# Unused identity transposes on TensorE at the entry of four stages of a four-layer language tower

## The chip, the cores and the metric

The kernel runs on one core of a Trainium2 chip. The metric is the device time of one execution in microseconds (us), the median of several runs. A core has five engines with queues of their own: PE (TensorE, with its weight loads shown as PEld), DVE (VectorE), ACT (ScalarE), POOL (GpSimd) and SP (SyncE, which here only starts transfers). They wait for each other through semaphores.

## The reference

256 tokens of 16 sequences pass through four layers, each a mixing part and a feed-forward part, with a residual around each (the first stage is an embedding with a convolution of nine taps over token ids):

```python
h = tok(x, emb, W, b)                                  # embedding and 9-tap convolution
h = h + linear_attention(layernorm(h))                 # L0
h = h + routed_ffn(layernorm(h))
h = h + batchnorm_attention(layernorm(h))              # L1
h = h + gelu_moe(layernorm(h), hidden=128, top2 of 8)
h = h + window_attention(layernorm(h))                 # L2
h = h + gelu_moe(layernorm(h), hidden=64, top2 of 8)   # keeps its input too
h = h + rational_convolution(layernorm(h))             # L3, by Fourier transforms
h = h + depth_ffn(layernorm(h))                        # upper half of the tokens by a router's weight
```

Shapes are (16, 256, 64) throughout, in fp32. The expert stages compute, for every token, a router's eight logits, keep the two largest with softmax weights, and add the two experts' outputs `gelu(x @ W1[e] + b1[e]) @ W2[e] + b2[e]`, weighted.

## The kernel before

The activations stay in one SBUF tensor `H`, as 8 chunks of 2 sequences x 256 tokens. Stages run one after the other (`tower`, the loop over `stages`, L2554), each in a block of its own with one queue of instructions per engine; between two blocks all engines meet at a barrier (L2563). PSUM is four tensors `PS[0..3]` of two banks each. Within a stage the order is written out by hand: semaphores carry every dependency, and what an engine does next is what its queue holds next.

**Expert stages** (`gelu_moe`, called as m1 with hidden 128, `again=True`, and as m2 with hidden 64, `again=False`). Each works in two rounds of four chunks. TensorE's queue opens with waits for the weights, for ScalarE's `sel` and for VectorE's `identb` and `b2_split` (L1271 to L1275). Then come, for the first round, `turn_x` twice (L1209: four 128x128 transposes of the normalised input each, with ScalarE's copy L1159 or L1162 between and after), `logits` (L1220: sixteen matmuls of 16 columns), `hidden(0)` and `hidden(1)` (L1237), `turn_parts` (L1226) and `gates(0)` (L1245). VectorE starts the stage with five small operations that split `b2` and one cast that makes `identb` (L1119), and then waits for the logits, from which a chain of 18 short operations (`Gating`, L966 to L991) makes the gates. From then on the loop over `steps` runs: gates (L1245), hidden (L1237), output (L1257, L1261), with ScalarE's Gelu (L1184) and VectorE's product (L1137) between. The banks: `hid_bank` is banks 0 to 2, `gate_bank` 3 and 4, `y_bank` 5 and 6, `ahead_bank` 7; `y_bank[1]` is first used by the second pair of chunks.

**Rational convolution.** TensorE waits for its weights and for VectorE's `nyq` (L2007), makes one transpose (L2008) that ScalarE copies (L1952) ahead of its sixteen L1954, and then waits for `coef` (L1871, a VectorE product). The loop of L2011 follows: four matmuls L2019 and L2022 (coefficients) and two L2030 (transform of the input) per step; ScalarE's L1965, L1966 and L1974 and VectorE's L1898 to L1906 take them up.

**Last stage** (`depth_ffn`). Its normalisation isn't prepared by the stage before: VectorE's statistics (L132 to L144), GpSimd's power (L150), VectorE's L156 and L166 come first. TensorE waits for `normed`, then runs, per round of four chunks, transposes L2242, router weights L2250, hidden L2258, output L2266, transposes L2275; ScalarE takes L2250's result with L2218, and VectorE ranks the tokens (L2160 to L2176) from it.

`C["ident"]` is the 128x128 identity in fp32, in SBUF since the start of the kernel (group `base`). `L2563` in the rows stands for the barrier between blocks, `PEq`, `DVEq`, `POOLq` for the engines' sequencers.

Of the kernel before, what the change touches and what calls it, by code (L numbers as in the profile page):

```python
# [21 lines left out]
P = 128  # L22
# [75 lines left out]

class NormBuffers:
# [902 lines left out]
def gelu_moe(nc, H, PS, C, dram, pre, hid, again):  # L1006
# [5 lines left out]
    with ExitStack() as ctx:  # L1012
# [20 lines left out]
        banks = [PS[k // 2][:, k % 2, :] for k in range(2 * W)]  # L1033
        hid_bank, gate_bank, y_bank, ahead_bank = banks[0:3], banks[3:5], banks[5:7], banks[7]
# [162 lines left out]
        def _(pe):  # L1197
            ident = C["ident"]
            w1 = C[pre + "_w1"].rearrange("p (s n) -> p s n", s=SL)
            w2 = C[pre + "_w2"].rearrange("p (s f) -> p s f", s=SL)  # L1200

            def turn_x(it, k):
                for w in (2 * k, 2 * k + 1):
                    pe.wait_ge(S["normed"], it * W + w + 1)
                    if k:
                        pe.wait_ge(S["xT"], it * 2 + 1)
                    for u in range(U):
                        at = (w % 2 * U + u) * P
                        ins = nc.tensor.transpose(ahead_bank[:, at:at + P],  # L1209
                                                  xn[:, w, 2 * u:2 * u + 2, :].rearrange("p g f -> p (g f)"), ident)  # L1210
                ins.then_inc(S["xT_ps"], 1)
# [566 lines left out]
def rational_convolution(nc, H, PS, C, dram):  # L1778
    with ExitStack() as ctx:
# [29 lines left out]
        banks = [PS[k // 2][:, k % 2, :] for k in range(2 * W)]  # L1809
# [189 lines left out]
        def _(pe):  # L1999
            ident = C["ident"]  # L2000
# [2 lines left out]
            odd = C["rat_odd"].rearrange("p (c n) -> p c n", c=2)  # L2003
            back = C["rat_back"].rearrange("p (t c u n) -> p t c u n", t=2, c=2, u=U)
            pe.wait_ge(C.sem("base"), C.count("base"))
            pe.wait_ge(C.sem("rat"), C.count("rat"))
            pe.wait_ge(S["nyq"], 7)  # L2007
            nc.tensor.transpose(banks[4][0:PAIRS, 0:P], nyq[:, 0], ident).then_inc(S["nyq_ps"], 1)  # L2008
# [31 lines left out]
            for m in range(PAIRS):  # L2040
# [4 lines left out]
                bank = banks[m % 8]  # L2045
# [9 lines left out]
            for l in range(LT):  # L2055
                bank = banks[l // 8 % 8]
# [45 lines left out]
def depth_ffn(nc, H, PS, C, dram):  # L2102
    with ExitStack() as ctx:
# [19 lines left out]
        @block.sync  # L2123
        def _(sp):

            ov = C.out.rearrange("(h c) (u p) f -> u h p c f", h=2, u=U)
            hv = H[:].rearrange("p (c u h f) -> p u h c f", c=CHUNKS, u=U, h=2)
            for r in range(ITERS):
                sp.wait_ge(S["h_new"], (r + 1) * W)
                for u in range(U):  # L2130
                    for half in range(2):
                        c = slice(r * W, (r + 1) * W)
                        sp.dma_start(ov[u, half][:, c], hv[:, u, half, c]).then_inc(S["stored"], 16)
            sp.wait_ge(S["stored"], 16 * U * 2 * ITERS)
# [95 lines left out]
        @block.tensor  # L2230
        def _(pe):
            ident = C["ident"]
            w1 = C["dep_w1"].rearrange("p (s h n) -> p s h n", s=SLABS, h=2)
            w2 = C["dep_w2"].rearrange("p (s f) -> p s f", s=SLABS)
            wr = C["dep_wr"].rearrange("p (h n) -> p h n", h=2)
            pe.wait_ge(C.sem("dep"), C.count("dep"))

            def one_round(it, first):
                for w in range(W):
                    pe.wait_ge(S["normed"], it * W + w + 1)  # L2240
                    for u in range(U):
                        ins = nc.tensor.transpose(PS[w][:, 0, u * P:(u + 1) * P],  # L2242
                                                  xn[:, w, 2 * u:2 * u + 2, :].rearrange("p g f -> p (g f)"), ident)
                    ins.then_inc(S["xT_ps"], 1)
                for w in range(W):
                    pe.wait_ge(S["xT"], it * W + w + 1)
                    if not first:
                        pe.wait_ge(S["ys"], (it - 1) * W + w + 1)
                    for half in range(2):
                        ins = nc.tensor.matmul(PS[w][:, 1, half * T:(half + 1) * T], wr[:, half, :], xT[:, w],  # L2250
                                               start=True, stop=True)
                    ins.then_inc(S["wb_ps"], 1)
                for w in range(W):
                    for s in range(SLABS):
                        if s == 1:
                            pe.wait_ge(S["wb"], it * W + w + 1)
                        for half in range(2):
                            ins = nc.tensor.matmul(PS[w][:, s, half * T:(half + 1) * T], w1[:, s, half, :], xT[:, w],  # L2258
                                                   start=True, stop=True)
                        ins.then_inc(S["hid0_ps"] if s == 0 else S["hid1_ps"], 1)  # L2260
                for w in range(W):
                    pe.wait_ge(S["hid0"], it * W + w + 1)
                    pe.wait_ge(S["hid1"], it * W + w + 1)
                    for half in range(2):
                        for s in range(SLABS):
                            ins = nc.tensor.matmul(PS[w][half * D:(half + 1) * D, 0, 0:T], w2[:, s, :],  # L2266
                                                   hid[:, w, s, half * T:(half + 1) * T], start=(s == 0),
                                                   stop=(s == SLABS - 1))
                    ins.then_inc(S["yT_ps"], 1)
                for w in range(W):  # L2270
                    pe.wait_ge(C.sem("base"), C.count("base"))
                    pe.wait_ge(S["yT"], it * W + w + 1)
                    for u in range(U):
                        at = slice(u * P, (u + 1) * P)
                        ins = nc.tensor.transpose(PS[w][:, 1, at], yT[:, w, at], ident)  # L2275
                    ins.then_inc(S["y_ps"], 1)

            one_round(0, True)
            with pe.Fori(1, ITERS) as it:
                one_round(it, False)  # L2280
# [306 lines left out]
```

## Time and profile before

| | us |
|---|---|
| median of 3 runs | 940.95 |
| lowest and highest run | 935.21 and 942.48 |
| the profiled execution's own time | 940.95 |
| its span, first to last instruction | 939.1 |
| PE busy | 696.9 (74%) |
| DVE busy | 517.8 (55%) |
| ACT busy | 341.9 (36%) |
| mean granted clock of TensorE | 0.813 of 2.4 GHz |

The page gives, per engine, busy time and its share of the span. The granted clock is that of TensorE alone and has two levels here, 0.50 (1.2 GHz) and 1.00 (2.4 GHz). In timelines an entry is: start, length, engine, line, operation, tensors, shape, count, and in brackets how long the engine sat idle before it and what released it. Matmuls are pipelined: their starts are recorded and their ends are modelled, so several in a row take less than the sum of their durations. An fp32 matmul of the program is two instructions in the trace, except for a transpose, which is one.

### The profile page before, as it was taken

The numbers are of one execution on the slowest core, as the hardware profiler recorded it, in microseconds if no ns is written. First come the engines' busy times: TensorE is split into PE (matmuls) and PEld (weight loads), VectorE is DVE, ScalarE is ACT, GpSimd is POOL, SyncE is SP. The second block draws the span as 40 slices with busy tenths as digits, with TensorE's granted clock in tenths as the row PEclk, the third lists the DMA queues.
The fourth block names the chain that finished last, engine by engine and source line by source line (L and its number), as shares of the span: only waits on it lengthen the run. The fifth ranks groups of instructions, "written<-read, shape, count | busy, mean of one in ns | idle before, by whom it ended". The sixth has DMA issues, their size and how long they took to land. (4 is left out here: it accounts for less than half of the span.)

```text
span 939.1 us, 13121 instructions
## 1 busy us (share of the span) xinstructions
PE 696.9 (74%) x4499; PEld 466.5 (50%) x4499; DVE 517.8 (55%) x1359; ACT 341.9 (36%) x620; POOL 217.1 (23%) x195
## 2 busy tenths in 40 slices
PE   2687667978882699984767777747876978999674
PEld 1565555647661323233656666633322645886453
DVE  0144883444547556752455545327375799444597
ACT  1232112425451245442333332212334967433253
POOL 6421110130201010102344434122013566000320
PEclk9899777988996599995667666555887999999788
DMA  8652221000000100000000000033000000000001
GB/s 278 177 158 76 77 63 59 2 1 1 1 1 0 60 1 1 1 14 22 6 6 6 7 6 6 6 116 138 0 1 31 1 0 1 1 2 1 1 21 26
DMA packets 18988, 32.31 MB, mean 34 GB/s; under 512 B 6482, under 2 KB 15730, under 8 KB 18162
## 3 DMA queue, kind: packets, MB, share of 16 engines
q1 hardware_dynamic: 16370, 22.11, 7.5%
q0 software_dynamic: 2560, 9.44, 3.2%
q8 instruction: 35, 0.57, 0.2%
q14 instruction: 23, 0.19, 0.1%
HBM read 29.54 MB, written 1.05 MB: 33 GB/s over the span
## 5 line engine op out<-in xcount | busy, mean ns | idle before, releaser
L150 POOL TENSOR_TENSOR norm_rstd<-norm_var,minus_half 128x16 f32<-128x16 f32 x16 | 47.1, 2942 | 367.2 <-DVE norm_var L144 367.2
L1184 ACT ACTIVATE m_g<-PS,w_slot 128x512 f32<-128x512 f32 x96 | 60.7, 685 | 72.2 <-PE PS L1237 65.9
L1137 DVE TENSOR_TENSOR m_gw<-m_g,PS 128x512 f32<-128x512 f32 x96 | 61.4, 683 | 41.8 <-PE PS L1245 29.6
L1237 PE MATMUL PS<-m_xT,w_slot 64*128 64x512 f32 x192 | 71.4, 702 | 6.9 <-ACT m_g L1184 6.8
L1261 PE MATMUL PS<-m_gw,w_slot 128*64 128x512 f32 x192 | 57.7, 671 | 0.0
L246 PE MATMUL PS<-w_base,tok_windows 128*128 128x128 f32 x128 | 22.0, 347 | 28.1 <-DMA tok_windows<-in_emb,tok_ids 18.5
L1409 POOL TENSOR_TENSOR win_rms<-win_ms,win_minus_half 128x24 f32<-128x24 f32 x8 | 33.3, 4167 | 37.4 <-DVE win_ms L1467 37.4
L1974 ACT COPY rat_xf<-PS 64x512 f32 x32 | 33.7, 1052 | 5.4 <-PE PS L2030 5.2
L1245 PE MATMUL PS<-m_gT,m_sel 48*128 48x512 bf16 x96 | 24.2, 425 | 15.3 <-DVE m_gw L1137 9.6
L226 POOL DMA_INDIRECT tok_windows<-in_emb,tok_ids x32 | 30.5, 952 | 21.5 <-PE PS L257 9.2
L1696 PE MATMUL PS<-win_v,win_probT 64*128 64x65 f32 x256 | 29.7, 405 | 7.5 <-ACT win_probT L1588 6.5
L246 PEld LDWEIGHTS PS<-w_base,tok_windows 128*128 128x128 f32 x128 | 19.9, 182 | 29.8 <-issue 16.2
L132 DVE BATCH_NORM_STATS2 norm_halves<-H 128x6 f32<-128x64 f32 x256 | 33.9, 210 | 0.9 <-PEq L2563 0.9
L2050 PE MATMUL PS<-w_slot,rat_ht 128*128 128x256 f32 x128 | 34.1, 391 | 0.0
L1464 DVE TENSOR_REDUCE win_ms<-win_sq 128x24 f32<-128x1536 f32 x8 | 14.0, 1753 | 35.6 <-ACT win_sq L1565 35.6
L1696 PEld LDWEIGHTS PS<-win_v,win_probT 64*128 64x128 f32 x256 | 28.0, 318 | 11.1 <-ACT win_probT L1588 9.5
L1237 PEld LDWEIGHTS PS<-m_xT,w_slot 64*128 64x128 f32 x192 | 24.3, 218 | 18.1 <-ACT m_g L1184 14.9
L2030 PE MATMUL PS<-w_slot 128*128 128x512 f32 x64 | 31.3, 613 | 0.3 <-DVE w_slot L1888 0.3
L1245 PEld LDWEIGHTS PS<-m_gT,m_sel 48*128 48x128 bf16 x96 | 5.4, 94 | 51.0 <-DVE m_gw L1137 27.8
L1261 PEld LDWEIGHTS PS<-m_gw,w_slot 128*64 128x64 f32 x192 | 10.3, 142 | 37.1 <-DVE m_gw L1137 26.4
L1906 DVE RECIPROCAL rat_hf<-rat_hf 128x256 f32<-128x256 f32 x16 | 27.9, 1741 | 0.0
L1920 DVE COPY rat_hf<-PS 128x512 f32 x16 | 16.6, 1040 | 20.0 <-PE PS L2050 20.0
(327 smaller groups left out, 1656.8 us busy)
## 6 DMA issues: line engine op xcount, KB each, us to landing
rff_routed<-in_routed SPq DMA_DIRECT2D x64, 129.0 KB, 2.1
rat_hf<-in_rat_den SPq DMA_DIRECT2D x1, 2048.0 KB, 7.6
rat_hf<-in_rat_num SPq DMA_DIRECT2D x1, 2048.0 KB, 13.5
w_slot<-in_w_rat SPq DMA_DIRECT2D x1, 1716.5 KB, 17.0
w_slot<-in_w_win SPq DMA_DIRECT2D x1, 1378.5 KB, 5.9
w_slot<-in_w_m SPq DMA_DIRECT2D x1, 1329.0 KB, 6.1
w_slot<-in_w_early SPq DMA_DIRECT2D x1, 1156.0 KB
out<-H SPq DMA_DIRECT2D x8, 128.0 KB, 2.2
```

The lines of the kernel that those rows point to most:

```text
L132: ins = nc.vector.bn_stats(N.st[:, w * G4 + g, :], x_of(w)[:, g, :])
L150: nc.gpsimd.tensor_tensor(N.rstd[:], N.var[:], C.minus_half[:], ALU.pow).then_inc(S["norm_rstd"], 1)
L246: ins = nc.tensor.transpose(PS[w][:, k, g * P:(g + 1) * P], win[:, slot(it, w), g, at:at + P], ident)
L1137: nc.vector.tensor_tensor(gw[:, i % 2, half, :], g[:, i % 2, half, :], gate_bank[half], ALU.mult)\
L1184: nc.scalar.activation(g[:, i % 2, half, :], hid_bank[(n - 1) % 3], ACT.Gelu, bias=b1[:, s:s + 1])\
L1237: nc.tensor.matmul(hid_bank[n % 3], w1[lane(half), s, :], pair_of(xT, pair)[lane(half)], start=True, stop=True).then_inc(S["hid_ps"], 1)
L1261: ins = nc.tensor.matmul(y[half], w2[:, s, :], gw[:, i % 2, half, :], start=False, stop=(s == SL - 1))
L1409: nc.gpsimd.tensor_tensor(rms[:, c % W], ms[:, c % W], minus_half[:], ALU.pow).then_inc(S["rms"], 1)
L1696: ins = nc.tensor.matmul(PS[w][:, i, g * DV:(g + 1) * DV], probT[rows[i], c % 2, half * (BLOCKS // 2) + g, :], (v if par else v2)[rows[i], ...
L1974: ins = nc.scalar.copy(dst, banks[4 + s % 4][rows, :].rearrange("p (t x l) -> p t x l", t=2, x=2))
L2030: ins = nc.tensor.matmul(banks[4 + s % 4], xd[:, w, 2 * u + half].rearrange("p a f -> p (a f)"), dft[:, u, :], start=(u == 0), stop=(u == ...
L2050: ins = nc.tensor.matmul(bank[:, 2 * LT:], part_of[c], odd[:, c, :], start=(c == 0), stop=(c == 1))
```

## The change

A helper `rouse` issues `count` transposes of the identity, each 128x128 fp32, into the first 128 columns of a bank that nothing uses at that time. They carry no semaphore, nothing reads their output, and they are issued in TensorE's queue ahead of the waits of the stage: 24 in the first expert stage, 44 in the second, 16 in the rational convolution (behind the wait for `base`, which is long met), 36 in the last stage. Nothing is removed or moved on any engine.

```diff
+def rouse(nc, C, bank, count):
+
+    for _ in range(count):
+        nc.tensor.transpose(bank[:, 0:P], C["ident"], C["ident"])
...
             w2 = C[pre + "_w2"].rearrange("p (s f) -> p s f", s=SL)
+            rouse(nc, C, y_bank[1], 24 if again else 44)
...
             pe.wait_ge(C.sem("base"), C.count("base"))
+            rouse(nc, C, banks[7], 16)
             pe.wait_ge(C.sem("rat"), C.count("rat"))
             pe.wait_ge(S["nyq"], 7)
...
             wr = C["dep_wr"].rearrange("p (h n) -> p h n", h=2)
+            rouse(nc, C, PS[3][:, 1, :], 36)
             pe.wait_ge(C.sem("dep"), C.count("dep"))
```

## Rows read from the trace of the kernel before

**Rows 1.** The page, part 1: busy us (share of the span) and instructions.

```profile
PE 696.9 (74%) x4499; PEld 466.5 (50%) x4499; DVE 517.8 (55%) x1359; ACT 341.9 (36%) x620; POOL 217.1 (23%) x195
```

**Rows 2.** The chain that ended last, last stage: start, us, what.

```profile
875.69 3.30 issue
...
879.03 3.03 POOL norm_rstd L150
...
885.40 5.31 PE PS L2250 x16
```

**Rows 3.** Timeline, PE, before and at the entry of the first expert stage.

```profile
294.14 4.14 PE L923 MATMUL PS<-w_base,bna_junk 128*128 128x128 f32 x16 [1.72 <-ACT bna_junk L835]
307.80 1.09 PE L1209 MATMUL PS<-w_base,norm_xn 128*128 128x128 f32 x4 [9.52 <-DVE m_identb L1119]
...
311.80 3.60 PE L1220 MATMUL PS<-w_slot,m_xT 128*128 128x16 f32 x16 [0.87 <-ACT m_xT L1159]
```

**Rows 4.** Timeline, DVE, entry of the first expert stage.

```profile
305.79 0.53 DVE L1076 CAST m_b2b<-w_slot 128x64 bf16<-128x64 f32 x1 [0.98 <-PEq L2563]
```

**Rows 5.** Timelines, DVE and PE, entry of the second expert stage.

```profile
626.18 0.54 DVE L1076 CAST m_b2b<-w_slot 128x64 bf16<-128x64 f32 x1 [1.59 <-PEq L2563]
...
629.95 1.09 PE L1209 MATMUL PS<-w_base,norm_xn 128*128 128x128 f32 x4 [5.86 <-DVE m_identb L1119]
```

**Rows 6.** Timeline, PE, other places: transposes and L1220 at either clock.

```profile
27.20 5.29 PE L246 MATMUL PS<-w_base,tok_windows 128*128 128x128 f32 x24 [2.99 <-DMA tok_windows<-in_emb,tok_ids]
38.45 3.68 PE L246 MATMUL PS<-w_base,tok_windows 128*128 128x128 f32 x16 [5.96 <-DVE tok_windowsT L302]
...
58.72 7.21 PE L246 MATMUL PS<-w_base,tok_windows 128*128 128x128 f32 x64 [0.77 <-DVE H L310]
...
660.36 0.66 PE L1209 MATMUL PS<-w_base,norm_xn 128*128 128x128 f32 x4
...
669.09 1.96 PE L1220 MATMUL PS<-w_slot,m_xT 128*128 128x16 f32 x16
```

**Rows 7.** Stretches: length, busy PE, PEld, DVE, ACT, POOL; then PEclk.

```profile
42.51:97.00 54.49, 45.71 (x327) 33.22 (x325) 24.52 (x78) 16.71 (x38) 11.56 (x10) 1.00 0.42 117
...
298.51:301.90 3.39, 0.00 (x0) 0.00 (x0) 3.29 (x20) 0.00 (x0) 1.53 (x1) 1.00 0.00 0
301.92:332.62 30.70, 19.37 (x58) 8.92 (x60) 16.59 (x67) 7.89 (x11) 4.78 (x3) 0.50 0.12 46
...
673.97:680.77 6.80, 4.83 (x10) 1.51 (x10) 2.16 (x5) 3.75 (x5) 0.00 (x0) 0.50 0.00 0
...
800.27:878.75 78.48, 70.02 (x793) 56.23 (x792) 34.28 (x84) 27.68 (x41) 0.00 (x0) 1.00 0.01 1
878.77:888.99 10.22, 6.05 (x17) 4.54 (x18) 7.66 (x33) 2.31 (x6) 7.51 (x6) 0.50 0.01 2
```

**Rows 8.** Timelines, DVE, PE and ACT, start of the rational convolution.

```profile
719.03 0.83 DVE L1859 TENSOR_TENSOR rat_hf<-w_slot 128x288 f32<-128x288 f32 x2 [1.10 <-PEq L2563]
...
721.69 0.37 PE L2008 MATMUL PS<-w_base,rat_nyq 128*32 128x128 f32 x1 [4.48 <-DVE rat_nyq L1869]
726.11 2.07 PE L2019 MATMUL PS<-rat_hf,w_slot 128*128 x4 [4.05 <-DVE rat_hf L1871]
...
722.60 8.42 ACT L1954 ACTIVATE rat_xf<-w_slot 128x512 f32<-128x512 f32 x16
...
732.85 1.05 ACT L1974 COPY rat_xf<-PS 64x512 f32 x1 [0.56 <-PE PS L2030]
```

**Rows 9.** Timeline, PE, first round of the last stage.

```profile
882.73 1.80 PE L2242 MATMUL PS<-w_base,norm_xn 128*128 128x128 f32 x6 [8.53 <-DVE norm_xn L166]
...
890.54 7.07 PE L2258 MATMUL PS<-dep_xT,w_slot 128*128 128x256 f32 x32
```

**Rows 10.** Timeline, PE, one step of the first expert stage, early and later.

```profile
326.00 1.20 PE L1245 MATMUL PS<-m_gT,m_sel 48*128 48x512 bf16 x2 [0.85 <-DVE m_gw L1137]
...
332.16 0.60 PE L1245 MATMUL PS<-m_gT,m_sel 48*128 48x512 bf16 x2
...
400.06 0.39 PE L1245 MATMUL PS<-m_gT,m_sel 48*128 48x512 bf16 x2
...
403.02 0.39 PE L1245 MATMUL PS<-m_gT,m_sel 48*128 48x512 bf16 x2
```

## The prediction

> **What bounds the kernel now.** I read four views, in this order. The page's busy shares first [rows 1]: the reader is to see that no engine is busy throughout; TensorE, the busiest, is at 74% and VectorE at 55%. So the kernel is a row of stages, each with its own chain of waits, and what TensorE's speed is worth has to be read stage by stage. Second, the chain that ended last [rows 2]. It reaches back only to the entry of the last stage; there TensorE counts with the sixteen L2250 matmuls (5.31 us), behind GpSimd's power (L150, 3.03 us). Third, the timelines at the four entries where the new work goes [rows 3, 4, 5, 8, 9]: what TensorE waits for there, and until when. Fourth, the granted clock by stretch [rows 7]: 1.00 is 2.4 GHz and 0.50 is 1.2 GHz. TensorE starts the first expert stage in a stretch of 0.50 that lasts from 301.92 to 332.62 us, though its real work begins at 307.80; the first round of the last stage falls into another, 878.77 to 888.99. The second expert stage starts at the low clock too: its L1209 takes the same 1.09 us [rows 3, 5].
>
> **What each transpose costs.** The new instruction is a 128x128 fp32 transpose, the form of L246 and L1209. 24 of L246 in a row took 5.29 us at the low clock and 64 took 7.21 us at the high one [rows 6]. The last one's pipeline overhangs, so I subtract L1209's four, 1.09 us cold [rows 3] and 0.66 fast [rows 6]: (5.29 - 1.09)/20 = 0.21 us each at 1.2 GHz, (7.21 - 0.66)/60 = 0.11 us each at 2.4 GHz.
>
> Do such transposes raise the clock? The L246 run that begins at 38.45 [rows 6] is followed by the high clock from 42.51 on [rows 7], 4.1 us later; and sixteen L923, from 294.14 to 298.28 [rows 3], are followed by 1.00 in 298.51:301.90 [rows 7]. Before both, TensorE had been idle or nearly so. So a run does raise it, some 4.1 to 4.4 us after it begins. And it does not stay: in 298.51:301.90 TensorE does nothing, and at 301.92 the clock is back at 0.50.
> The Trainium skill (TensorE: Matmul & The Clock Gate, Part 4: PE-mode transpose) says the opposite, that transposes don't engage the full clock. By that rule nothing would be gained anywhere and the sum would be rival B's; the two runs above contradict it.
>
> **First expert stage (24).** All engines enter at about 305.8 (VectorE's first row [rows 4]). Today TensorE waits until 307.80, for VectorE's small casts that end with m_identb [rows 3]. So 2.0 us of the new work is covered, the rest delays L1209. Bounds: all 24 cold are 24 x 0.21 = 5.0 us, 3.0 past the cover; all fast are 2.6 us, 0.6 past it. By the rise above I take 4.1 us cold (19 or 20 transposes) and 5 x 0.11 = 0.55: 4.6 us, +2.6 us. What is queued behind is all of it: L1209, ScalarE's copy, L1209 again, L1220, and then VectorE's gate chain, which can't start before L1220. Against that, what runs at the high clock right after: twice four L1209, 1.09 to 0.66 us, 2 x 0.43 = 0.86; sixteen L1220, 3.60 to 1.96 us [rows 3, 6], 1.64. Together 2.5 us. Net +0.1 us; +3.0 - 0.86 = +2.1 if the clock rises late and falls before L1220.
> Then, from the end of L1220 at 315.4 [rows 3] to the gates' work at 326.00 [rows 10], TensorE has little beside VectorE's gate chain, and I expect the clock to fall. The rows say so: in the second expert stage L1220 ran fast at 669.09 (1.96 us) [rows 6], two L1237 followed, and the stretch 673.97:680.77 is at 0.50 [rows 7]. So the PE-bound first step, 326.00 to 332.16 [rows 10], stays as slow as it is.
>
> **Second expert stage (44).** The entry is at 626.2, the real L1209 at 629.95 [rows 5]: 3.8 us of cover, more because VectorE's casts are slower here. 4.1 us cold (19) and 25 x 0.11 = 2.75 make 6.85 us, +3.05 past the cover. Bounds: 44 x 0.21 = 9.2 us, +5.4; all fast 4.8 us, +1.0. Gain: the same L1209, 0.86, and L1220, up to 1.64. L1220 begins some 3 us after L1209, with TensorE half idle between; I take half of it here, 0.8. Net +3.05 - 1.7 = +1.3 us.
>
> **Convolution (16).** Entry at 719.0 [rows 8]. 16 x 0.21 = 3.4 us, to 722.4; the transpose L2008 stood at 721.69, so it comes 0.7 us late. Behind it wait ScalarE's copy and its sixteen L1954, which run from 722.60 for 8.42 us without a gap; ScalarE had 0.56 us idle before L1974 at 732.85 [rows 8]. 0.7 - 0.56 = 0.15 us late, which the small gaps of the next steps take up. TensorE's own next work waits for VectorE until 726.11 [rows 8], so it idles again, as it did before the fall at 301.92. Even with the clock held, ScalarE is the one that sets the first step, so the gain is at most those 0.56 us. I take 0; bounds -0.56 and +0.7.
>
> **Last stage (36).** The clock is at 1.00 until 878.75 [rows 7] and the entry is at about 875.7 [rows 2], so the run begins fast: 36 x 0.11 = 4.0 us, to 879.7. If the clock fell inside, at most 36 x 0.21 = 7.6 us, to 883.3, 0.6 past the first L2242 at 882.73 [rows 9]. Cover: GpSimd's power and VectorE's L166. I take 0 for the cost. Gain: the chain holds L2250 with 5.31 us; at the high clock sixteen would take half of L2258's 7.07 us for 32 [rows 9], 3.5, so at most 1.8 us. But 3 us idle follow, and then L2242 in pairs, each waiting for VectorE. By the 301.92 fall I expect the low clock to be back before L2250: 0 here, bound -1.8.
>
> **Sum.** +0.1 + 1.3 + 0 + 0 = +1.4 us on the profiled execution's own 940.95 us (span 939.1 and 1.85 around it; it is also the median of the three): 942.4 us.
>
> **Rivals.**
> (A) The clock holds once raised. Then the first step of both expert stages is fast as well: 326.00 to 332.16 is 6.2 us, the same work from 400.06 to 403.02 is 3.0 us [rows 10], 3.2 us each. First stage +0.1 - 3.2, second +3.05 - 2.5 - 3.2 = -2.65, convolution -0.56, last -1.8: -8.1 us, 932.8. For it: the work after a run is not nothing. Against it: the fall at 301.92 and the one at 673.97. A part of it, one stretch of the four, gives 938 to 941.
> (B) The clock isn't raised, because the operand is the identity, mostly zeros, where L246 and L923 carried data. Then +3.0 and +5.4 for the expert stages and +0.15 for the convolution, nothing in the last stage: +8.6 us, 949.5. It decides as soon as the spacing of the new transposes stays at 0.21 us to their end. For it: no row shows an identity on both sides; against it: the runs of [rows 3, 6]. The Trainium skill (TensorE: Matmul & The Clock Gate, Part 4: PE-mode transpose) would bring the same.
> (C) The clock rises, but falls before L1220: first stage +2.1, second +3.05 - 0.86 = +2.2, convolution +0.7: +5.0 us, 946.0. For it: TensorE is half idle between the two L1209 groups and L1220, which wait for ScalarE's copies.
> Where a rise or a fall comes isn't fixed to the program, and the three runs of before differ by 7.3 us; so each term has a scatter of a us or two that I can't sign.
>
> **How the numbers follow.** Forecast (+1.4, with small shifts either way, 938 to 944.5) 0.56; a part of A 0.14; A itself 0.07; C 0.15; B 0.08. The range that holds 8 in 10 takes in the forecast, part of A and most of C: 936 to 947. 1% is 9.4 us, about what a measurement of this kernel can tell from no change. Faster by over that (under 931.5) needs all of A and more: 0.06. Slower (over 950.4) needs B with a scatter on top: 0.05. Within: 0.89.
>
> **What would show it.** L1209's first start moves some 2.6 us after the new run's cover in the first expert stage and 3 in the second; the spacing of the new transposes falls from 0.21 to 0.11 within the run; L1209's four take 0.66 and L1220 about 2 us; the stretch before the first PE-bound step is at 0.50 again. In the convolution L2019's first instruction stays 7.1 us after the entry. In the last stage L2250 still takes over 4.6 us. I am wrong if the clock reads 1.00 when the gates (L1245) begin, if L2250 takes 3.5 us, or if the new run never speeds up.

## The result and the profile after

The changed kernel takes 936.06 us (median of 20 runs) against 940.45 us for the kernel before (20 runs of its own beside them): a ratio of 0.9961, 95% interval [0.9943, 0.9979]. The medians differ by 4.4 us, a small gain, just inside the predicted range (by 0.1 us) but on the other side of the kernel before than the forecast (+1.4 us). The ratio, which leaves out two slow executions of the changed kernel (1000.33 and 3367.49 us), isn't the quotient of the medians (0.9953): it stands for 3.7 us. The profiled execution takes 936.7 us (span 934.9), 4.2 less than the one before. The mean granted clock is 0.836, before it was 0.813.

The page of the changed kernel, part 1, and two groups of part 5 (line, operation, busy us and mean ns of one, then idle time before them and what ended it). L1244 and L1268 were L1237 and L1261 before: the helper and its calls moved the later lines by 6 to 9.

```profile
PE 700.0 (75%) x4619; PEld 475.3 (51%) x4619; DVE 516.7 (55%) x1359; ACT 341.6 (37%) x620; POOL 217.8 (23%) x195
...
L1244 PE MATMUL PS<-m_xT,w_slot 64*128 64x512 f32 x192 | 68.3, 667 | 7.6 <-ACT m_g L1190 7.5
L1268 PE MATMUL PS<-m_gw,w_slot 128*64 128x512 f32 x192 | 55.7, 649 | 0.0
```

The same groups of the kernel before, part 5 of its page.

```profile
L1237 PE MATMUL PS<-m_xT,w_slot 64*128 64x512 f32 x192 | 71.4, 702 | 6.9 <-ACT m_g L1184 6.8
L1261 PE MATMUL PS<-m_gw,w_slot 128*64 128x512 f32 x192 | 57.7, 671 | 0.0
```

There are 120 instructions more, the new ones, and nothing else differs [rows 1]. These two groups, which both expert stages share, became 5.1 us shorter on TensorE (3.1 and 2.0); the stretches below show more of the work at the high clock.

The first question is where. I take the length of a stage from one barrier to the next, in each profiled execution (us). The mark is the moment at which GpSimd clears the semaphores inside the barrier, about half a us ahead of the stage's first rows:

| kernel | up to 1st expert | 1st expert | window attention | 2nd expert | convolution | last |
|---|---|---|---|---|---|---|
| before | 305.2 | 114.9 | 205.4 | 93.0 | 156.8 | 63.4 |
| changed | 307.1 | 114.2 | 202.9 | 90.9 | 158.1 | 61.4 |

Up to the first expert stage the change touches nothing; its +1.9 is scatter between executions. The window attention has no new work and is 2.5 us shorter; the convolution is 1.3 longer. Timeline of PE in the changed kernel, entries of the four stages.

```profile
307.66 4.26 PE L106 MATMUL PS<-w_base 128*128 128x128 f32 x24 [7.51 <-PEq L2572]
311.76 0.60 PE L1216 MATMUL PS<-w_base,norm_xn 128*128 128x128 f32 x4
...
314.82 1.96 PE L1227 MATMUL PS<-w_slot,m_xT 128*128 128x16 f32 x16 [0.87 <-ACT m_xT L1165]
...
327.38 1.20 PE L1252 MATMUL PS<-m_gT,m_sel 48*128 48x512 bf16 x2 [0.85 <-DVE m_gw L1143]
...
624.72 6.64 PE L106 MATMUL PS<-w_base 128*128 128x128 f32 x44 [2.09 <-PEq L2572]
631.19 0.60 PE L1216 MATMUL PS<-w_base,norm_xn 128*128 128x128 f32 x4
...
633.86 2.66 PE L1227 MATMUL PS<-w_slot,m_xT 128*128 128x16 f32 x16 [0.68 <-ACT m_xT L1168]
...
645.67 0.61 PE L1252 MATMUL PS<-m_gT,m_sel 48*128 48x512 bf16 x2 [1.51 <-DVE m_gT L1096]
...
715.48 1.94 PE L106 MATMUL PS<-w_base 128*128 128x128 f32 x16 [1.82 <-PEq L2572]
...
722.57 2.07 PE L2027 MATMUL PS<-rat_hf,w_slot 128*128 x4 [4.16 <-DVE rat_hf L1878]
...
873.63 4.12 PE L106 MATMUL PS<-w_base 128*128 128x128 f32 x36 [1.63 <-PEq L2572]
880.54 1.80 PE L2251 MATMUL PS<-w_base,norm_xn 128*128 128x128 f32 x6 [2.78 <-DVE norm_xn L172]
882.99 4.17 PE L2259 MATMUL PS<-dep_xT,w_slot 128*128 128x256 f32 x16
```

L106 is the new run; the reader is to see how long it takes (24 in 4.26 us, 44 in 6.64), that what follows at once is fast (L1216 in 0.60, 1.09 before [rows 3]) and that the first gates' work at 327.38 is as slow as before, 1.20 us for two L1252 [rows 10]. Stretches of the changed kernel in the two expert stages (length, then busy PE, PEld, DVE, ACT, POOL, then PEclk):

```profile
310.80:317.40 6.60, 4.77 (x39) 4.06 (x38) 0.47 (x2) 1.55 (x2) 0.00 (x0) 1.00 0.25 105
317.55:334.50 16.95, 12.59 (x32) 3.44 (x31) 12.63 (x53) 5.29 (x8) 2.90 (x1) 0.50 0.00 1
...
628.12:634.90 6.78, 5.34 (x48) 4.89 (x46) 0.00 (x1) 1.17 (x2) 0.00 (x0) 1.00 0.99 425
634.97:651.98 17.01, 13.38 (x36) 5.05 (x37) 13.05 (x55) 5.29 (x8) 1.21 (x1) 0.50 0.31 133
...
658.85:662.20 3.35, 3.35 (x11) 1.32 (x10) 0.00 (x0) 0.51 (x2) 0.00 (x0) 0.50 0.00 0
...
675.95:682.70 6.75, 6.12 (x14) 2.17 (x16) 2.31 (x5) 2.42 (x4) 0.00 (x0) 0.50 0.00 0
682.75:716.70 33.95, 25.80 (x127) 8.51 (x124) 22.39 (x64) 11.65 (x19) 4.17 (x2) 1.00 0.02 3
```

The high clock won by the new run is gone at 317.5 and at 635.0, before the PE-bound part of either stage begins. But the second stage's later half, from 682.75 to its end at 715.5, runs at 1.00 throughout. Stretches of the kernel before, same columns, same part of the second expert stage:

```profile
687.63:691.02 3.39, 3.39 (x10) 0.50 (x8) 1.25 (x2) 1.35 (x3) 0.00 (x0) 0.50 0.02 5
691.04:701.25 10.21, 7.86 (x40) 2.31 (x38) 6.94 (x30) 4.27 (x7) 0.59 (x1) 1.00 0.00 0
701.28:708.08 6.80, 6.80 (x16) 1.77 (x16) 4.34 (x9) 1.85 (x3) 2.29 (x1) 0.50 0.00 0
```

Here the clock is at 0.50 twice, 10.2 us in all (3.4 and 6.8), and TensorE is busy through both. In both kernels a long low stretch ends 27.3 us into the stage. From there to the stage's end it had 17.0 us at 0.50 before (these and the 6.8 of [rows 7]) and has 10.1 after (658.85 and 675.95). 6.9 us less at half speed, where TensorE is the limit, are worth up to 3.4 us; the gates begin 0.8 later; the stage is 2.1 shorter. So the time is found. What brought it there, 50 us behind the new work, is the question for the experiments.

### The profile page after: what moved, and what is told of

Its sections match the earlier page's. It is cut to its first block and busy times, and to the rows that moved or that the text cites. A ratio compares the mean times of both kernels' runs of the same rounds, so it can differ in the third digit from the quotient of the medians.

```text
span 934.9 us, 13361 instructions
## 1 busy us (share of the span) xinstructions
PE 700.0 (75%) x4619; PEld 475.3 (51%) x4619; DVE 516.7 (55%) x1359; ACT 341.6 (37%) x620; POOL 217.8 (23%) x195
## 5 line engine op out<-in xcount | busy, mean ns | idle before, releaser
L1143 DVE TENSOR_TENSOR m_gw<-m_g,PS 128x512 f32<-128x512 f32 x96 | 61.3, 683 | 38.1 <-PE PS L1252 24.5
L1244 PE MATMUL PS<-m_xT,w_slot 64*128 64x512 f32 x192 | 68.3, 667 | 7.6 <-ACT m_g L1190 7.5
L1268 PE MATMUL PS<-m_gw,w_slot 128*64 128x512 f32 x192 | 55.7, 649 | 0.0
L252 PE MATMUL PS<-w_base,tok_windows 128*128 128x128 f32 x128 | 21.2, 339 | 29.2 <-DMA tok_windows<-in_emb,tok_ids 18.4
L1252 PE MATMUL PS<-m_gT,m_sel 48*128 48x512 bf16 x96 | 24.5, 418 | 16.6 <-DVE m_gw L1143 10.8
L232 POOL DMA_INDIRECT tok_windows<-in_emb,tok_ids x32 | 30.5, 952 | 21.9 <-PE PS L263 9.4
L1703 PE MATMUL PS<-win_v,win_probT 64*128 64x65 f32 x256 | 27.2, 378 | 8.1 <-ACT win_probT L1595 7.1
L1244 PEld LDWEIGHTS PS<-m_xT,w_slot 64*128 64x128 f32 x192 | 23.7, 211 | 18.1 <-ACT m_g L1190 15.3
L1703 PEld LDWEIGHTS PS<-win_v,win_probT 64*128 64x128 f32 x256 | 25.6, 292 | 11.2 <-ACT win_probT L1595 9.6
L1252 PEld LDWEIGHTS PS<-m_gT,m_sel 48*128 48x128 bf16 x96 | 5.6, 94 | 50.2 <-DVE m_gw L1143 32.9
L1268 PEld LDWEIGHTS PS<-m_gw,w_slot 128*64 128x64 f32 x192 | 10.2, 139 | 35.4 <-DVE m_gw L1143 24.4
```

The source lines that it names most:

```text
L252: ins = nc.tensor.transpose(PS[w][:, k, g * P:(g + 1) * P], win[:, slot(it, w), g, at:at + P], ident)
L1143: nc.vector.tensor_tensor(gw[:, i % 2, half, :], g[:, i % 2, half, :], gate_bank[half], ALU.mult)\
L1244: nc.tensor.matmul(hid_bank[n % 3], w1[lane(half), s, :], pair_of(xT, pair)[lane(half)], start=True, stop=True).then_inc(S["hid_ps"], 1)
L1268: ins = nc.tensor.matmul(y[half], w2[:, s, :], gw[:, i % 2, half, :], start=False, stop=(s == SL - 1))
L1703: ins = nc.tensor.matmul(PS[w][:, i, g * DV:(g + 1) * DV], probT[rows[i], c % 2, half * (BLOCKS // 2) + g, :], (v if par else v2)[rows[i], ...
```

## The experiments

Two theories at the outset. **Warmth:** what the new transposes warm up is paid back, at once or later. **Shift:** the transposes only delay the stage, and the clock then falls over other work; warm or cold doesn't matter, and the sign hangs on the size of the delay. Counts are written (first expert, second expert, convolution, last stage); the changed kernel is (24, 44, 16, 36). Each ratio is against the kernel before on the same chip; where a count is 0, the call stands with 0 in it and issues nothing. The lengths quoted are those of one profiled execution each, by the method above.

**The parts alone.**

```diff
 e1_m1 (24, 0, 0, 0)
-            rouse(nc, C, y_bank[1], 24 if again else 44)
+            rouse(nc, C, y_bank[1], 24 if again else 0)
...
 e2_m2 (0, 44, 0, 0)
-            rouse(nc, C, y_bank[1], 24 if again else 44)
+            rouse(nc, C, y_bank[1], 0 if again else 44)
...
 e4_dep (0, 0, 0, 36)
-            rouse(nc, C, y_bank[1], 24 if again else 44)
+            rouse(nc, C, y_bank[1], 0 if again else 0)
...
```

> Only the first expert stage has its 24 transposes. Theory 1: the stage takes about 114.2 instead of 114.9 us, ratio 0.9990 to 0.9995. Theory 2 (the recorded sum): +0.1 us, 115.0 us. The two hardly differ in the time; they differ in whether the first product of the gates (L1245) starts earlier or later after the entry: 20.2 us before, 19.7 after.

Measured: 940.05 against 942.04 us, ratio 0.9975 [0.9951, 0.9999]. First expert stage 114.8, window attention 205.8 us: its trace shows no gain. That execution took 942.80 us at a mean granted clock of 0.812, and seven of the other eleven had 0.826 to 0.833, so what made the median smaller isn't in this trace.

> Only the second expert stage has its 44 transposes. Theory 1 (local gain as between the two profiles): the stage takes about 91 instead of 93 us, ratio about 0.998. Theory 2 (the recorded sum): L1209 starts 2.5 to 3 us later than entry + 3.8, L1209 and L1220 give back 1.7 to 2.5 of it, the stage takes 93 to 94.5 us and the ratio is 1.000 to 1.0015.

Measured: 940.18 against 942.04, 0.9981 [0.9959, 1.0004]. Second expert stage 90.9, convolution 158.1, last stage 61.3 us: the three lengths of the changed kernel, though the convolution and the last stage have no new work here. This execution took 935.03 us, the second fastest of its twelve.

> Only the last stage has its 36 transposes. Theory 1 (gain is real and local: the clock rises earlier in the stage that has the new work): the last stage, 63.4 us in the profile before and 61.4 in the one after, takes 61 to 62 us, L2250's sixteen take about 4.2 instead of 5.3 us, and the whole is 1.5 to 2.5 us faster (ratio 0.9975 to 0.9985). Theory 2 (the recorded one: the clock falls before L2250, the difference of the two profiles is where rises happen to come): the stage scatters around 63 us and the ratio's interval holds 1.

Measured: 942.52 against 942.04, 1.0003 [0.9986, 1.002]. Last stage 63.4 us, as before. PE timeline of e4_dep, entry of the last stage:

```profile
880.96 4.12 PE L106 MATMUL PS<-w_base 128*128 128x128 f32 x36 [1.63 <-PEq L2572]
887.87 1.80 PE L2251 MATMUL PS<-w_base,norm_xn 128*128 128x128 f32 x6 [2.78 <-DVE norm_xn L172]
890.32 5.50 PE L2259 MATMUL PS<-dep_xT,w_slot 128*128 128x256 f32 x16
```

A stretch of e4_dep behind the new run:

```profile
887.35:894.10 6.75, 6.04 (x17) 4.52 (x18) 6.05 (x28) 2.29 (x6) 4.46 (x5) 0.50 0.00 1
```

Thirty-six transposes in 4.12 us, 2.8 us idle, and the clock is at 0.50 when L2251 begins. And e2_m2, with no new work in this stage, has the short L2259 of the changed kernel (PE timeline of e2_m2):

```profile
878.88 1.80 PE L2251 MATMUL PS<-w_base,norm_xn 128*128 128x128 f32 x6 [8.53 <-DVE norm_xn L172]
881.34 4.17 PE L2259 MATMUL PS<-dep_xT,w_slot 128*128 128x256 f32 x16
```

What follows: the transposes of the last stage do nothing that a profile shows. Those of the convolution were never run alone, but it takes 158.1 us with them (changed) and without them (e2_m2). The lengths of both stages come from something that happens ahead of them. By the medians the two expert parts carry the gain, each about half (-2.0 and -1.9 us), though e2_m2's interval still holds no change at all and that of e1_m1 ends just short of it.

**Cold filler of the same place.** To part warmth from delay, the body of the helper becomes a matmul of 16 columns, which is two instructions of 0.21 us. TensorE is as busy as in the cold part of the real run; in the traces of these three kernels the clock stayed at 0.50 through it in the expert stages.

```diff
-        nc.tensor.transpose(bank[:, 0:P], C["ident"], C["ident"])
+        nc.tensor.matmul(bank[:, 0:16], C["ident"], C["ident"][:, 0:16], start=True, stop=True)
 e5_narrow (10, 15, 6, 12); e10_shift11 (0, 11, 0, 0); e11_shift13 (0, 13, 0, 0)
```

> All four places have filler of about the same length in time, but made of matmuls of 16 columns (10, 15, 6 and 12 of them, each two instructions of about 0.21 us cold). In the trace before, sixteen such instructions (L1220) in a row were not followed by the high clock. Theory 1 (the clock is what gains): no rise after the filler, L1209 and L1220 stay slow, both expert stages lose about 2.3 and 2.6 us, and the whole is 4 to 6 us slower than before (ratio 1.004 to 1.006). Theory 3 (something else gains, such as a place in the queue or a moved instruction load): about as fast as the changed kernel, 0.996.

Measured: 944.94 against 942.04, 1.0032 [1.0012, 1.0052]. PE timeline of e5_narrow, first expert stage:

```profile
308.01 4.42 PE L106 MATMUL PS<-w_base 128*128 128x16 f32 x20 [7.67 <-PEq L2572]
312.27 1.09 PE L1216 MATMUL PS<-w_base,norm_xn 128*128 128x128 f32 x4
316.28 3.60 PE L1227 MATMUL PS<-w_slot,m_xT 128*128 128x16 f32 x16 [0.87 <-ACT m_xT L1165]
```

Nothing is warmed: 1.09 and 3.60 us as in [rows 3]. The two expert stages take 117.0 and 94.3, but the window attention 202.8, the convolution 158.1 and the last stage 61.3, as in the changed kernel. Taken whole, a cold filler costs time. That showed two effects of opposite sign rather than one, so I matched the delay of a single stage, to 0.1 us.

> Only the second expert stage has filler, eleven matmuls of 16 columns (22 instructions, about 4.7 us). They don't raise the clock, and they hold L1216 back by about 0.9 us past the cover of 3.8, so that the gates' first product comes 0.9 us late, as it does with the 44 transposes (0.8). Theory 2 (the delay alone moves the later rounds to where the clock falls less often; the early rise isn't what gains): the stage takes 90.5 to 92 us, the convolution about 158.1 and the last stage 61.3, and the ratio is 0.996 to 0.999 although nothing was warmed. Theory 1 (the early rise of the clock is what gains): the delay is lost, the stage takes 93.5 to 94.3 us, the ratio is 1.000 to 1.003.

Measured: 940.19 against 941.75, 0.9985 [0.9961, 1.001]. PE timeline of e10_shift11, second expert stage:

```profile
626.30 4.84 PE L106 MATMUL PS<-w_base 128*128 128x16 f32 x22 [2.09 <-PEq L2572]
630.99 1.09 PE L1216 MATMUL PS<-w_base,norm_xn 128*128 128x128 f32 x4
634.61 3.60 PE L1227 MATMUL PS<-w_slot,m_xT 128*128 128x16 f32 x16 [0.68 <-ACT m_xT L1168]
647.35 0.61 PE L1252 MATMUL PS<-m_gT,m_sel 48*128 48x512 bf16 x2 [1.51 <-DVE m_gT L1096]
```

The last stretch of that stage in e10_shift11:

```profile
684.45:718.40 33.95, 24.55 (x116) 7.25 (x112) 22.39 (x65) 11.67 (x19) 4.22 (x2) 1.00 0.01 2
```

L1216 and L1227 are cold, yet the gates begin at 647.35, 21.05 us into the stage, against 20.95 in the changed kernel (from VectorE's first row of the stage), and from 684.45 on the clock is at 1.00 to the end. Stages: 90.9, 158.2, 61.4 us. From the second expert stage on that is 310.5 us, 310.4 in the changed kernel and 313.1 before: all of those 2.7 us but 0.1, without a warm transpose. The timed runs agree in size (-1.6 us, beside -1.9 for e2_m2), but neither interval excludes zero: the control is shown in the profiled executions and not by the medians.

> As the run with eleven, with thirteen such matmuls (about 5.6 us, L1216 1.8 us late). Theory 2: another length again, anywhere from 91 to 94.5 us, not eleven's plus 0.9. Theory 1: eleven's plus 0.9 us.

Measured (one execution): 945.48 us. Two matmuls more than e10, the gates at 21.9 us, 0.8 later, and the stage takes 96.4 us, 5.5 more. Stretches of e11_shift13:

```profile
692.40:695.70 3.30, 3.30 (x11) 0.59 (x8) 1.05 (x2) 1.47 (x3) 0.00 (x0) 0.51 0.00 0
...
706.00:712.70 6.70, 6.70 (x16) 1.69 (x15) 4.20 (x9) 1.85 (x3) 2.14 (x1) 0.50 0.00 0
```

The two falls of the kernel before are back, 3.5 us later in the stage.

**Warm runs of other lengths in the second expert stage.** The counts are (0, 24, 0, 0), (0, 34, 0, 0) and (0, 60, 0, 0).

```diff
+            rouse(nc, C, y_bank[1], 0 if again else 24)
+            rouse(nc, C, y_bank[1], 0 if again else 34)
+            rouse(nc, C, y_bank[1], 0 if again else 60)
```

> Only the second expert stage, with 24 instead of 44 transposes: 4.6 us, 0.8 past the cover of 3.8, against 2.7 past it with 44. Theory 1 (what gains is the early rise of the clock; the delay costs): L1216 starts 1.9 us earlier than with 44, the stage is about 1 to 2 us shorter than with 44, 89 to 90 us. Theory 2 (what gains is the place that the later rounds of the stage come to stand at against the clock's rises and falls, which a delay of 0.8 us moves): no such order; the stage jumps to 93 us or more, or stays at 90.9, and convolution and last stage come as 156.8 with 63.4 or as 158.1 with 61.3.

Measured: 938.42 against 941.1, 0.997 [0.9948, 0.9993]. The profiled execution, 934.41 us, is the second fastest of its twelve.

> 34 transposes in the second expert stage alone: by the rate of 0.11 us after the rise L1216 starts 1.1 us earlier than with 44. Theory 2: the length is not 44's minus 1.1; with 24 it was 91.1, with 44 it was 90.9, and a value between them in the count may give 90 as well as 94. Theory 1: 90.0 us or less.

Measured (one execution): 937.38 us.

> 60 transposes in the second expert stage alone: L1216 starts 1.8 us later than with 44, and the clock stays up a stretch longer (L1227 all fast). Theory 2: the length jumps or stays, 90.9 to 95 us. Theory 1: 44's 90.9 plus 1.8 minus at most 0.7, about 92 us.

Measured (one execution): 946.02 us.

PE timelines of the three: the new run, which begins at the stage's entry, and the first gates' work. First e7_m2_24:

```profile
622.40 4.45 PE L106 MATMUL PS<-w_base 128*128 128x128 f32 x24 [2.09 <-PEq L2572]
...
640.46 0.61 PE L1252 MATMUL PS<-m_gT,m_sel 48*128 48x512 bf16 x2 [1.51 <-DVE m_gT L1096]
```

The same of e12_m2_34:

```profile
625.38 5.55 PE L106 MATMUL PS<-w_base 128*128 128x128 f32 x34 [2.09 <-PEq L2572]
...
644.53 0.61 PE L1252 MATMUL PS<-m_gT,m_sel 48*128 48x512 bf16 x2 [1.51 <-DVE m_gT L1096]
```

The same of e13_m2_60:

```profile
627.82 8.38 PE L106 MATMUL PS<-w_base 128*128 128x128 f32 x60 [2.09 <-PEq L2572]
...
649.80 0.61 PE L1252 MATMUL PS<-m_gT,m_sel 48*128 48x512 bf16 x2 [1.51 <-DVE m_gT L1096]
```

Side by side, all the profiled executions (e6, e8 and e14 to e16 are described further down):

| second expert stage | gates begin, us after VectorE's first row | length, us |
|---|---|---|
| none (before, e9, e1, e4) | 20.11 to 20.15 | 92.9 to 93.0 |
| 24 warm (e7, e14) | 18.06, 18.07 | 91.1 |
| 34 warm (e12, e15) | 19.15, 19.18 | 90.9, 90.8 |
| 44 warm (changed, e16, e2, e6) | 20.92 to 20.96 | 90.8 to 90.9 |
| 11 narrow, cold (e10) | 21.05 | 90.9 |
| 44 warm and 14 more (e8) | 21.15 | 94.1 |
| 13 narrow, cold (e11) | 21.89 | 96.4 |
| 60 warm (e13) | 21.98 | 96.4 |
| 15 narrow, cold (e5) | 22.76 | 94.3 |

Delays that agree to 0.1 us give equal lengths, whether the filler was warm or cold (44 and 11 narrow; 60 and 13 narrow), and the length isn't a rising function of the delay. With 24 warm transposes the gates come 2.1 us earlier and the stage is 1.9 us shorter, so they pay for themselves at the gates. Whether the 1.9 us come from that isn't shown: with 34 the gates are 1.0 earlier, with 44 they are 0.8 later, and the stage is no longer for it.

**Both expert stages, and keeping the clock up.** e6 is (24, 44, 0, 0). e8 is e6 with six more transposes ahead of the first wait for Gelu and eight behind the first `turn_parts`, where TensorE is idle, to carry the clock to the gates.

```diff
 e8_fill
+                    if n == 3:
+                        rouse(nc, C, y_bank[1], 6)
...
+            rouse(nc, C, y_bank[1], 8)
```

> The transposes of the two expert stages alone (24 and 44), none in the convolution and the last stage. In the profiles so far the last stage took 63.4 us both without and with its own 36, and 61.3 us with no working filler at all, always together with a convolution of 158.1 us; so its length seems to follow from the stage before. Theory 1 (the expert stages make the whole gain, the last two edits nothing): ratio 0.995 to 0.998, as the changed kernel's 0.9961; second expert stage 90.9, convolution 158.1, last stage 61.3 us. Theory 2 (each of the four edits carries a part): ratio 0.998 to 0.999 and a last stage of 63.4 us.

Measured: 938.39 against 941.1, 0.9964 [0.9936, 0.9993]: the whole gain of the change within the uncertainty, without the convolution's and the last stage's part. PE timeline of e6_experts, first expert stage:

```profile
306.94 5.36 PE L106 MATMUL PS<-w_base 128*128 128x128 f32 x24 [7.67 <-PEq L2572]
312.09 0.87 PE L1216 MATMUL PS<-w_base,norm_xn 128*128 128x128 f32 x4
...
315.41 3.06 PE L1227 MATMUL PS<-w_slot,m_xT 128*128 128x16 f32 x16 [0.87 <-ACT m_xT L1165]
```

In this execution the clock rose only 5.7 us after the run began, all 24 were cold, and the stage took 117.3 us in place of 114.2. The code of the stage is the same, the moment of the rise is another: 3.1 us.

> The expert stages' transposes (24 and 44) and further ones where TensorE idles before the first products of the gates: 6 ahead of the wait for the first Gelu in hidden(1), 8 between turn_parts and the wait for gT. Theory 1 (the clock has fallen by the first PE-bound step, which takes 6.2 us cold and 3.0 fast in the rows of before): the step gets faster by 1 to 3 us in both stages, and the whole is 2 to 6 us faster than with 24 and 44 alone. Theory 2 (there is too little idle time to fill, the transposes delay the Gelu's matmuls): the first step is still slow and both stages lose 0.2 to 1 us each.

Measured: 940.22 against 941.1, 0.9992 [0.9967, 1.0017]. PE timeline of e8_fill, second expert stage (L1254 is its gates' line):

```profile
637.80 1.54 PE L106 MATMUL PS<-w_base 128*128 128x128 f32 x6
...
641.68 1.91 PE L106 MATMUL PS<-w_base 128*128 128x128 f32 x8
643.52 0.61 PE L1254 MATMUL PS<-m_gT,m_sel 48*128 48x512 bf16 x2
644.98 1.20 PE L1254 MATMUL PS<-m_gT,m_sel 48*128 48x512 bf16 x2 [0.85 <-DVE m_gw L1143]
```

The additional ones ran cold and the gates are slow all the same. They delay the gates by 0.2 us, and the stage takes 94.1 us, 3.2 more than in e6. So what the clock did at the gates wasn't mended. Whether the 3.2 us come from the delay alone no run separates, since the fourteen also stand between other work of the stage.

**The kernel before once more, and the counts on one chip.** e9_before has the code of before. e14, e15 and e16 ran together on another chip, where the first stage is some 10 us shorter in every trace: (24, 24, 0, 0), (12, 34, 0, 0), and the changed kernel again.

```diff
+            rouse(nc, C, y_bank[1], 24)
+            rouse(nc, C, y_bank[1], 12 if again else 34)
```

> The kernel before once more, for a second trace of it. Theory 1 (the entry of the second expert stage finds the clock's rises and falls in the same place each time, so that the stage's length is a property of its own code): second expert stage 93.0, convolution 156.8, last stage 63.4 us again, and 114.8 us in the first expert stage. Theory 2 (all stage lengths are drawn by chance): other values, 90.9 us for the second expert stage among them.

Measured (one execution): 938.55 us; expert stages and what follows 114.8, 205.3, 93.0, 156.8, 63.4 us, each within 0.1 of the first profile. The 2.4 us between the two executions of one code lie ahead of the first expert stage (303.1 against 305.2, 2.1 us).

> 24 transposes in both expert stages, none elsewhere. Theory 2 (place against the clock's falls): the second expert stage, convolution and last stage take 91.1, 158.0 and 61.3 us as with 24 there alone, the same 310.4 as with 44; so the ratio is that of the changed kernel, 0.995 to 0.998. Theory 1 (each us of earlier gates is a us gained): the gates start 2.9 us earlier than with 44, ratio about 0.993.

Measured: 925.33 against 930.01 (8 runs), 0.9941 [0.9918, 0.9963]. The stages came as theory 2 has it: the gates of the second expert stage begin 2.9 us earlier than with 44, and it takes 91.1 us all the same. The ratio lies between the two theories and decides neither.

> 12 transposes in the first expert stage and 34 in the second, none elsewhere. 12 take 2.5 us cold, 0.4 past the cover of 2.1, and may or may not raise the clock. Theory 2: first expert stage with window attention 317 or 320 us in the trace, whichever way the gates come to stand; second expert stage on, 310.4 us; ratio 0.995 to 0.999. Theory 1: the first expert stage loses the rise and gains nothing, the second as with 44; ratio 0.998.

Measured: 926.8 against 930.01, 0.997 [0.9951, 0.9988]. The 12 took 2.79 us, and the clock stayed at 0.50 behind them.

> The changed kernel once more, beside the two others on one chip. Theory 2: second expert stage 90.9, convolution 158.1, last stage 61.3 us again; the first expert stage gives 114.2 us with window attention 202.9 where its entry stands to the clock as in the first trace, and other lengths where it doesn't. Theory 1: all stages as in the first trace.

Measured: 928.42 against 930.01, 0.9969 [0.9945, 0.9992]. Again a gain: the medians differ by 1.6 us, the ratio is that of 2.9.

48 transposes in place of 120 do as well within the uncertainty: the two intervals overlap, and the profiled stages of e14 and e16 are equal to 0.3 us each (114.2, 202.8, 91.1, 158.0, 61.3 and 114.2, 202.8, 90.8, 158.2, 61.3), so a lead of e14 isn't shown. With 12 in the first expert stage it stays at 114.9 and the window attention at 204.8.

**The window attention.** It has no edit in any kernel. Nine profiled executions without new work in the first expert stage give it 205.3 to 205.9 us. With 24 transposes there, four of six give 202.6 to 202.9 (changed, e16, e14, e8) and two 205.8 to 205.9 (e1, e6); with the cold filler (e5) it is 202.8, and with 12 transposes (e15) 204.8. A stretch over the whole stage, kernel before:

```profile
420.60:626.10 205.50, 143.72 (x1146) 120.72 (x1146) 91.12 (x189) 59.27 (x105) 71.31 (x63) 0.62 0.03 9
```

The same of the changed kernel:

```profile
421.70:624.60 202.90, 140.17 (x1146) 117.76 (x1146) 90.69 (x189) 59.25 (x105) 71.29 (x63) 0.66 0.03 9
```

The same 1146 instructions, a mean clock of 0.66 in place of 0.62, 3.6 us less on TensorE. That is the largest single term of the changed profile, and nothing in the stage was touched.

## Why the prediction was wrong in sign

**Cost and speed of a transpose.** Right. The spacing fell from 0.21 to 0.11 us within the run, 24 took 4.26 us and 44 took 6.64, where 4.65 and 6.85 were predicted; 44 cold would be 9.2, so rival B is out. One reading under it was not sound: the recorded clock begins at 32.26 us, and so no row shows the low clock for the 24 L246 from 27.20; it was inferred from their spacing. The 24 of e6, at a granted clock of 0.50 throughout, took 5.36 us and bear the 0.21 out. The rise came 3.0 and 3.4 us into the run, earlier than my 4.1, and once, in e6, 5.7. The Trainium skill (TensorE: Matmul & The Clock Gate, Part 4: PE-mode transpose) has it that transposes don't engage the full clock; the trace of the changed kernel disagrees: 1.00 in 628.12:634.90, which sets in 3.4 us into a run of transposes begun at the low clock.

**First expert stage.** L1216 moved by 2.1 us (2.6 predicted); the gates came 0.5 us earlier, where +0.1 was the forecast. With the late rise of e6 they came 1.9 later, near the bound of +2.1.

**Second expert stage, entry.** L1216 moved by 2.7 us (3.05 predicted), L1227 took 2.66 us where 2.8 was assumed, and the gates came 0.8 late, not 1.3. The term was 0.5 too large. The clock fell inside L1227 here, so rival C came half true, and at 0.8 us and not 2.2.

**The clock falls before the PE-bound step.** Right, both times (317.55 and 634.97), and e8_fill couldn't hold it. Rival A, the only way to a large gain that I saw, did not happen. The gain came without it.

**Convolution and last stage at nothing.** Right for the new work as far as the profiles show: e4_dep gives 1.0003, and e2_m2 has the lengths of the changed kernel without it. The 16 transposes took 1.94 us and not 3.4, since the clock was still at 1.00 at that entry; L2027 stayed 7.1 us after it, as predicted. L2259 took 4.17 us, below the 4.6 that I had set as a sign, but it does so in e2_m2 too.

**The step that failed** is the sum. It carries the entry's +1.3 us unchanged to the end of the second expert stage, and takes every other stage at its old length but for its own small term. I had written that "each term has a scatter of a us or two that I can't sign", as if it belonged to the execution.

For the second expert stage and the two behind it that isn't so in the profiled executions: kernels with the same delay there have the same length of the stage to 0.1 us (93.0, 90.9, 96.4), and the changed kernel's lengths came back in e16 on another chip. For the first expert stage it is: with 24 transposes it took 114.2 us four times, and 114.8 (e1) and 117.3 (e6). A shift of 0.8 us moves the rounds of the second expert stage against the places where the clock falls, and the next stages' entries too.

In the profile the terms are -2.1 (second expert), +1.3 (convolution), -2.0 (last stage), -2.5 (window attention), -0.7 (first expert): -6.0 in all; with the +1.9 ahead of them that is the -4.2 of the execution's own time, to a rounding of 0.1. The forecast had these at +1.3, 0, 0, 0 and +0.1. e10_shift11 shows in its trace that the first three need the delay alone. For the window attention only e5 speaks for that; why e1 and e6 miss the short form isn't settled. That they do, and that the medians of the changed kernel (-4.4 us, on the other chip -1.6) are smaller than the profile's -6.0, says that one execution overstates what holds on the average. So does e5_narrow: its profiled stages from the first expert on add up to 633.5 us like those of before, and its median is 2.9 us slower. The profiled executions of e2 and e7 are each the second fastest of twelve, so their lengths needn't be the usual ones.

What stays open: how much of the medians' -4.4 us is warmth that pays and how much is favourable placement. Warmth is shown to bring the gates forward for 24 transposes at an entry (0.5 and 2.1 us). For the 44 of this change it is not what gained in the traces: there the gates are later, and a cold delay does the same. What sets the window attention's length, the largest term, stays open.

## What to carry to other kernels

Warm TensorE up only where its real work follows without a gap, and by no more than brings the clock up: here 24 transposes did as well as 44, and those ahead of a wait of 3 us were worth nothing. When a profile shows falls of the clock over PE-bound work, a small shift at the entry of the stage can matter more than what is warmed (here gates 0.8 us later went with a stage 2.1 us shorter, gates 1.8 later with one 3.4 longer); before crediting an edit with such a gain, run a control that delays the stage equally and does nothing else. Such a gain belongs to the placement, and another edit in the same stage can take it away: with the fourteen more of e8 the 90.9 us were 94.1.

## What the runs showed that I had not expected

- The second expert stage's length went 91.1, 90.9, 93.0, 90.9, 94.1, 96.4, 94.3 us as its gates began at 18.1, 19.2, 20.1, 21.0, 21.2, 21.9 and 22.8 us: steps of 2 to 3 us, up and down, for shifts of 0.1 to 1 us (the 94.1 is e8, which has further edits in the stage).
- In e10_shift11 TensorE was busy with 16-column matmuls for 4.8 us and four transposes behind them, and the granted clock stayed at 0.50; in e5_narrow it stayed there through 7.4 us in which TensorE was never idle (627.90 to 635.30). In the runs of 24 and more 128x128 transposes at the same spacing it rose 2.7 to 5.7 us after the first.
- Executions of the same code differ in mean granted clock, and their time follows it: over 35 runs of the kernel before on one chip from 0.807 to 0.826 and 937.9 to 946.5 us, correlation -0.71, a least-squares slope of -3.7 us per 0.01.
